# A graph layer and a ternary feed-forward layer on one core: ten weight groups made ternary by GpSimd, and a new order around the last neighbour sums and the first units

## The chip, the cores and the metric

One core of a Trainium2 chip runs the whole program. The time is the device time of one execution in microseconds (us), and of several runs the median is quoted. Engines are named as in the profile: PE is TensorE (PEld its weight loads), DVE is VectorE, ACT is ScalarE, POOL is GpSimd and SP is SyncE, whose queue issues most DMAs.

## What is computed

Inputs are x (1250 nodes x 512), 20000 edges src to dst sorted by dst, two 512 x 512 matrices and a bias for the graph layer, and three weight matrices for the feed-forward layer (gate and up 1408 x 512, down 512 x 1408), all float32.

```python
# graph layer, on xl = layernorm(x)
neigh = segment_sum(xl[src], dst) / maximum(deg, 1)
h = xl @ W_self + neigh @ W_neigh + b
h = where(h >= 0, h, 0.01 * h)
x = x + h / maximum(sqrt(sum(h * h, axis=1)), 1e-12)
# feed-forward layer, on xl = layernorm(x); every weight matrix quantized in groups of 128:
scale = mean(abs(group)) + 1e-5
wq = clip(round(group / scale), -1, 1) * scale
x = x + (silu(xl @ wq_gate.T) * (xl @ wq_up.T)) @ wq_down.T
```

## The kernel before

Everything is written out by hand: each engine's program is one Python function that emits instructions in order, and engines meet only through counting semaphores. Each engine executes its own list strictly in order. The nodes lie in NT = 10 tiles of 125 rows.

**The first stretch, 80 slots.** For each tile PE multiplies the normalized and transposed x (xnT) with W_neigh and W_self (w_sb), eight products of 512 columns, one a slot. Between them it builds the adjacency matrix a_t (1250 x 1250 counts) from one-hot rows: 157 chunks of 128 edges, two a slot. DVE makes the one-hot rows, hot_dst (add_chunk on PE waits for each) and, for eight chunks at once, hot_src. ACT copies finished blocks from PSUM into a_t, the products into y_hi and z, and the transposed x into xnT; DVE makes y_lo, the rest that y_hi leaves. The weights are quantized in the same slots. SP loads them in 34 loads of up to four groups (128 x 128) into four slots of raw; 22 of gate and up, 12 of down. For each group (a job) ACT takes magnitudes and their sum (abs_of: mag, absum), POOL makes a threshold for a load (scales_of: thr), and DVE makes the ternary weight times its magnitude (ternary_of), of which only the sign is used later:

```python
nc.vector.scalar_tensor_tensor(out=tq_of(j), in0=mag_of(j), scalar=thr[:, j:j + 1], in1=raw_of(j),
                               op0=ALU.is_gt, op1=ALU.mult).then_inc(ternary, 1)
```

There are two slots of mag, so ACT's first job of load l waits until the ternaries of load l - 2 are made, and SP's load l until those of l - 4. Loads 0 to 22 are made in the slots, loads 23 to 33 in the neighbour sums.

**The neighbour sums, n = 0 to 9.** PE multiplies a_t with y_hi and y_lo (ten pairs of 512 columns a tile, banks 4 and 5 in turn). POOL has added the bias to z. DVE reads the sum (neighbour_sum: z), applies the leaky step (leak), makes the inverse norm of tile n - 1 and adds it to x (residual: nrm, inv, x_sb, then bn and mv, the statistics), finishes the normalization factors of tile n - 2 (shift1), makes x1_lo of tile n - 3 and the ternaries of the loads that ACT did in n - 1 (down_jobs). ACT squares z, takes roots and normalizes x (normalize1: xn) for tile n - 2; PE transposes tile n - 3 behind tile n, and ACT and DVE split it into x1_hi and x1_lo.

**The units, n = 0 to 32 and three more.** A unit is a row f of 128 hidden features and a third c of the nodes (376, 376 or 500 columns). Each has eight pieces, G0 to G3 and U0 to U3 (one group of gate or up each, x1_hi and x1_lo), and four pieces D0 to D3 (down), which come three units later. The pieces go through seven banks (RING); the matmul of a piece waits until the piece seven before is taken from its bank. ACT takes G0, U0, D1 and D3 and DVE the others, both times nscale. ACT makes silu (sg), POOL the product hh, ACT h_hi and POOL h_lo. The signs of the weights of row f are made by ACT (ternary_out) from a transposition, of row 0 through bank 7 by PE, of most others by DMA. Bank 7 also takes the transpositions of tiles 7, 8 and 9; the table BANK7 says after which piece each comes.

## Time and profile before

| | |
|---|---|
| median of 3 runs | 340.61 us (340.24 to 342.66) |
| the profiled execution | 338.97 us, its span 337.2 us |
| PE busy | 317.1 us (94%) |
| DVE busy | 299.7 us (89%) |
| ACT busy | 236.9 us (70%) |
| POOL busy | 169.3 us (50%) |

The span runs from the first to the last instruction of the profile, and what lies around it makes up the 1.8 us to the time of that execution. Busy times of PE come from modelled ends of pipelined matmuls, so they say where PE has gaps, and not how fast it works. Everything below is from this one execution.

### The profile page before, as it was taken

To read this page: it belongs to the slowest core of one execution; us is meant where nothing else is said; L and a number is where in the kernel's file an instruction comes from. 1 tells how busy PE (TensorE), PEld (TensorE's weight loads), DVE (VectorE), ACT (ScalarE), POOL (GpSimd) and SP (SyncE) were. 2 spreads that over 40 slices of the span, in tenths; PEclk is the share of its full clock that TensorE was granted. 3 is DMA by queue.
4 is the path that set the end of the run, shared out by engine and by line. 5 is a ranking of instruction groups with operands and counts; after the bars stand their busy time and mean duration, and the time that the engine had idled before them with its cause. 6 is when DMAs were issued, how large, how long until landed. Compare 5 with 4: busy or idle time off the path is not lost.

```text
span 337.2 us, 5722 instructions
## 1 busy us (share of the span) xinstructions
PE 317.1 (94%) x1521; PEld 239.6 (71%) x1521; DVE 299.7 (89%) x782; ACT 236.9 (70%) x636; POOL 169.3 (50%) x235
## 2 busy tenths in 40 slices
PE   8999999999999998889879999999999999999991
PEld 3444455454555786668659898998989988899981
DVE  3699999999994399998799999999999999999993
ACT  2188988789882357864778786867878688676750
POOL 6025000010102950100015596989889897899992
PEclk9999999999999999999979999999999999999998
DMA  7992322232320021311001111111110100000305
GB/s 211 285 233 68 91 62 65 65 92 83 84 82 25 4 62 54 90 27 24 9 21 25 27 24 29 24 25 28 24 26 16 23 2 1 2 1 1 118 7 182
DMA packets 23610, 19.62 MB, mean 58 GB/s; under 512 B 15230, under 2 KB 16084, under 8 KB 23576
## 3 DMA queue, kind: packets, MB, share of 16 engines
q1 hardware_dynamic: 23498, 19.16, 21.4%
q8 instruction: 13, 0.21, 0.3%
q14 instruction: 21, 0.17, 0.2%
q10 hardware_dynamic: 78, 0.08, 0.1%
HBM read 13.73 MB, written 2.56 MB: 48 GB/s over the span
## 4 chain that ended last, share of the span: by engine, by line
PE 56%; DVE 25%; issue 6%; POOL 5%; DMA 3%; ACT 2%; SPq 1%; DVEq 0%; ACTq 0%; POOLq 0%
PE bank L1409 44%; DVE hot_dst L1098 4%; PE bank L1306 4%; POOL z L719 4%; DVE tq_gu L999 4%; DVE tq_d L999 3%; PE bank L1343 3%; DMA x_sb<-in_x 3%; DVE hot_src L1089 2%; DVE bn L985 1%; DVE bn L1154 1%; DVE x_sb L1151 1%; PE bank L1258 1%; PE bank L1247 1%; DVE z L1133 1%
## 5 line engine op out<-in xcount | busy, mean ns | idle before, releaser
L1409 PE MATMUL bank<-x_hi,t_gu 128*128 128x376 f32 (+1 forms) x264 | 94.8, 359 | 1.5 <-ACT t_gu L875 0.8
L1409 PE MATMUL bank<-x_lo,t_gu 128*128 128x376 f32 (+1 forms) x264 | 93.5, 354 | 0.0
L1306 PE MATMUL bank<-w_sb,xnT 128*125 128x512 f32 x160 | 82.9, 606 | 0.5 <-ACT z L823 0.3
L1206 DVE SCALAR_TENSOR_TENSOR g_acc<-bank,nscale,g_acc 128x376 f32<-128x376 f32 (+1 forms) x99 | 64.0, 646 | 4.6 <-PE bank L1409 3.2
L1206 DVE SCALAR_TENSOR_TENSOR u_acc<-bank,nscale,u_acc 128x376 f32<-128x376 f32 (+1 forms) x99 | 63.8, 645 | 0.2 <-issue 0.2
L732 POOL TENSOR_TENSOR acc<-acc,d_one 128x376 f32<-128x376 f32 (+1 forms) x58 | 63.6, 1101 | 0.0
L679 POOL TENSOR_SCALAR thr<-absum 128x4 f32<-128x4 f32 (+1 forms) x34 | 9.6, 282 | 98.3 <-ACT mag_early L789 74.6
L742 POOL TENSOR_TENSOR hh<-sg,u_acc 128x376 f32<-128x376 f32 (+1 forms) x32 | 35.2, 1100 | 45.2 <-ACT sg L926 45.1
L1409 PEld LDWEIGHTS bank<-x_hi,t_gu 128*128 128x128 f32 x264 | 50.3, 191 | 6.6 <-issue 1.0
L1409 PEld LDWEIGHTS bank<-x_lo,t_gu 128*128 128x128 f32 x264 | 50.3, 190 | 3.4
L1258 PEld LDWEIGHTS bank<-hot_dst,hot_src 128*126 128x126 bf16 x157 | 20.6, 135 | 40.7 <-DVE hot_dst L1098 25.8
L1409 PE MATMUL bank<-h_hi,t_d 128*128 128x376 f32 (+1 forms) x132 | 47.4, 359 | 0.1
L1409 PE MATMUL bank<-h_lo,t_d 128*128 128x376 f32 (+1 forms) x132 | 46.6, 353 | 0.0
L1343 PE MATMUL bank<-y_hi,a_t 125*125 125x512 f32 x100 | 40.1, 401 | 0.8 <-DVE a_t L1055 0.8
L1206 DVE SCALAR_TENSOR_TENSOR acc<-bank,nscale,acc 128x376 f32<-128x376 f32 (+1 forms) x62 | 39.4, 643 | 0.5 <-POOL acc L732 0.5
L1343 PE MATMUL bank<-y_lo,a_t 125*125 125x512 f32 x100 | 39.4, 394 | 0.0
L751 POOL TENSOR_TENSOR h_lo<-hh,h_hi 128x376 fp32r<-128x376 f32 (+1 forms) x32 | 35.1, 1098 | 3.1 <-ACT h_hi L948 2.5
L905 ACT ACTIVATE d_one<-bank,nscale 128x376 f32<-128x376 f32 (+1 forms) x58 | 34.8, 604 | 1.7 <-PE bank L1409 1.7
L1098 DVE TENSOR_SCALAR hot_dst<-iota_w,key 128x140 bf16<-128x140 uint16 (+4 forms) x150 | 34.5, 271 | 0.9 <-PE bank L1258 0.8
L789 ACT ACTIVATE mag_early<-raw 128x128 f32<-128x128 f32 x92 | 27.5, 304 | 7.7 <-DVE tq_gu L999 6.5
L999 DVE SCALAR_TENSOR_TENSOR tq_gu<-mag_early,thr,raw 128x128 bf16<-128x128 f32 x88 | 28.9, 354 | 2.8 <-POOL thr L679 2.7
L905 ACT ACTIVATE g_acc<-bank,nscale 128x376 f32<-128x376 f32 (+1 forms) x33 | 20.0, 607 | 16.0 <-PE bank L1409 15.2
(140 smaller groups left out, 545.6 us busy)
## 6 DMA issues: line engine op xcount, KB each, us to landing
raw<-in_L_ffn_w_gate SPq DMA_DIRECT2D x11, 256.0 KB, 2.7
raw<-in_L_ffn_w_up SPq DMA_DIRECT2D x11, 256.0 KB, 2.6
out_x<-x_sb SPq DMA_DIRECT2D x10, 224.0 KB
raw<-in_L_ffn_w_down SPq DMA_DIRECT2D x8, 256.0 KB, 2.6
turned<-tq_gu SPq DMA_TRANSPOSE x80, 2.4
w_sb<-in_L_gnn_W_neigh SPq DMA_DIRECT2D x1, 1024.0 KB, 6.1
w_sb<-in_L_gnn_W_self SPq DMA_DIRECT2D x1, 1024.0 KB, 7.6
x_sb<-in_x SPq DMA_DIRECT2D x2, 448.0 KB
```

The source lines that it names most:

```text
L732: nc.gpsimd.tensor_tensor(to, to, d_one[:, o, slot, 0:width(u)], ALU.add).then_inc(d_added, 1)
L742: nc.gpsimd.tensor_tensor(hh[:, u % 2, 0:w], sg[:, u % 2, 0:w], u_acc[:, u % 2, 0:w], ALU.mult).then_inc(h_done, 1)
L751: nc.gpsimd.tensor_tensor(h_lo[:, u % h_slots, 0:w], hh[:, u % 2, 0:w], h_hi[:, u % h_slots, 0:w].bitcast(F32), ALU.subtract).then_inc(hlo ...
L789: nc.scalar.activation(mag_of(j), raw_of(j), ACT.Abs, accum_out=absum[:, j:j + 1]).then_inc(abs_done, 1)
L905: nc.scalar.activation(to, bank_of(u, what)[:, 0:width(u)], ACT.Copy, scale=nscale[:, j:j + 1]).then_inc(act_took, 1)
L999: nc.vector.scalar_tensor_tensor(out=tq_of(j), in0=mag_of(j), scalar=thr[:, j:j + 1], in1=raw_of(j), op0=ALU.is_gt, op1=ALU.mult).then_inc ...
L1098: nc.vector.tensor_scalar(to, numbers, key[:, c:c + 1], None, ALU.is_equal).then_inc(hot_made, 1)
L1206: nc.vector.scalar_tensor_tensor(out=to, in0=bank_of(u, what)[:, 0:w], scalar=nscale[:, j:j + 1], in1=to, op0=ALU.mult, op1=ALU.add).then_ ...
L1258: nc.tensor.matmul(bank[k % 3][0:TQ, 0:NT * WIN].rearrange("p (s d) -> p s d", d=WIN)[:, :, lo:hi], hot_src[:, c // SB % SBS, c % SB, 0:TQ ...
L1306: last = nc.tensor.matmul(to[0:TP, :], xnT[:, t, k * TP:(k + 1) * TP], w_sb[:, k, half * D:(half + 1) * D], start=k == 0, stop=k == KD - 1)
L1343: last = nc.tensor.matmul(bank[4 + n % 2][0:TP, :], a_t[0:TP, s, n * TP:(n + 1) * TP], y[:, s, :], start=s == 0 and y is y_hi, stop=s == N ...
L1409: last = nc.tensor.matmul(bank_of(u, what)[:, 0:width(u)], w, parts[h], start=h == 0, stop=h == 1)
```

## The change

POOL makes the ternaries of ten of the 34 loads, 38 of 132 groups, in two steps (ternary_group); everybody who waited for the counter of ternaries now waits for two counters (wait_ternary). POOL's bias additions are dealt out over the tiles. In the neighbour sums PE's transpositions come a tile later, inside the tile after its first three pairs. DVE makes the residuals of tiles 7 and 8 in their own turn, and POOL that of tile 9. The signs of row 0 go to a place of their own (t_gu0), over data of the edges that are no longer used, where they are made before the last sum is read. RING and BANK7 change, and ACT's takes, normalizations and splits at the start of the units come in another order; DVE's inverse norm of tile 9 comes after the take of G2, and its statistics in unit 1.

```diff
+    t_gu0 = place("t_gu0", [P, 2, D], F32R, "small", edge_data)
+        POOL_LOADS = (6, 10, 14, 18, 22, 24, 26, 28, 30, 32)
+
+        def wait_ternary(engine, j):
+
+            done = [l for l in range(len(loads)) if load_end[l] <= j]
+            assert load_end[done[-1]] == j
+            mine = sum(loads[l][1] for l in done if l not in POOL_LOADS)
+            pools = sum(l in POOL_LOADS for l in done)
+            engine.wait_ge(ternary, mine)
+            if pools:
+                engine.wait_ge(ternary_pool, pools)
-        RING = [2, 6, 4, 5, 3, 1, 0]
+        RING = [2, 6, 4, 1, 0, 5, 3]
-        BANK7 = {(0, "U2"): ("T", 1, 0), (0, "U3"): ("X", 7), (1, "U2"): ("X", 8), (1, "U3"): ("T", 0, 1), (2, "U1"): ("X", 9),
+        BANK7 = {(0, "U2"): ("T", 1, 0), (0, "G1"): ("X", 7), (2, "U0"): ("X", 8), (2, "U3"): ("T", 0, 1), (3, "G0"): ("X", 9),
+            def ternary_group(l):
+
+                n = loads[l][1]
+                js = slice(load_end[l] - n, load_end[l])
+                if l < 2 * NF:
+                    to = tq_gu[:, l, :]
+                else:
+                    o, f = down_order[js.start - 2 * NF * KD]
+                    to = tq_d[:, o, f * P:(f + n) * P]
+                mag = (mag_early if l < LOADS1 else mag_late)[:, l % MAGS, 0:n * P]
+                pool.wait_ge(scales, l + 1)
+                for i, j in enumerate(range(js.start, js.stop)):
+                    m = mag[:, i * P:(i + 1) * P]
+                    nc.gpsimd.tensor_scalar(m, m, thr[:, j:j + 1], None, ALU.is_gt).then_inc(mags_over, 1)
+                pool.wait_ge(mags_over, sum(loads[p][1] for p in POOL_LOADS if p <= l))
+                nc.gpsimd.tensor_tensor(to, mag, raw[:, l % RAWS, 0:n * P], ALU.mult).then_inc(ternary_pool, 1)
...
-            for t in range(NT):
+            def add_bias(t):
+
                 pool.wait_ge(z_out, t + 1)
                 nc.gpsimd.tensor_tensor(z[:, t, :], z[:, t, :], bias_b[0:TP, :], ALU.add).then_inc(z_done, 1)
-            for l in range(LOADS1, len(loads)):
-                scales_of(l)
+
+            for t in range(4):
+                add_bias(t)
+            for n in range(NT):
+                if n + 4 < NT:
+                    add_bias(n + 4)
+                for l in down_loads_in(n):
+                    scales_of(l)
+                    if l in POOL_LOADS:
+                        ternary_group(l)
...
+            t = NT - 1
+            pool.wait_ge(inv_done, 2 * t + 2)
+            nc.gpsimd.tensor_scalar(z[:, t, :], z[:, t, :], inv[0:TP, t:t + 1], None, ALU.mult).then_inc(h_unit, 1)
+            pool.wait_ge(h_unit, 1)
+            nc.gpsimd.tensor_tensor(x_sb[:, t, :], x_sb[:, t, :], z[:, t, :], ALU.add).then_inc(x1_done, 1)
...
+                    if s == 3 and n >= 4:
+                        transpose_x1(n - 4)
...
-                if 3 <= n:
-                    t = n - 3
-                    if t >= 2:
-                        pe.wait_ge(xlo_done, t - 1)
-                    transpose_xn(t, normed1, x1_bank(t), x1n_T, place_of(t)[2])
-                if n == NT - 2:
+                if n == NT - 1:
+                    transpose_x1(n - 3)
+                if n == NT - 3:
                     pe.wait_ge(rdeg_done, 4)
                     ternary_in(0, 0)
```

On POOL, from the last thresholds of the first stretch on (thr) through the bias additions (z) into the down loads: before,

```order
L679 TENSOR_SCALAR thr<-absum 128x4 x19
L719 TENSOR_TENSOR z<-z,bias_b 125x512 x10
L679 TENSOR_SCALAR thr<-absum 128x3
L679 TENSOR_SCALAR thr<-absum 128x4 x2
L679 TENSOR_SCALAR thr<-absum 128x3
L679 TENSOR_SCALAR thr<-absum 128x4 x3
L679 TENSOR_SCALAR thr<-absum 128x3
```

and now, beginning with the product of load 22,

```order
L722 TENSOR_TENSOR tq_d<-mag_early,raw 128x512
L766 TENSOR_TENSOR z<-z,bias_b 125x512 x5
L705 TENSOR_SCALAR thr<-absum 128x3
L705 TENSOR_SCALAR thr<-absum 128x4
L720 TENSOR_SCALAR mag_late<-mag_late,thr 128x128 x4
L722 TENSOR_TENSOR tq_d<-mag_late,raw 128x512
L766 TENSOR_TENSOR z<-z,bias_b 125x512
L705 TENSOR_SCALAR thr<-absum 128x4
L705 TENSOR_SCALAR thr<-absum 128x3
L720 TENSOR_SCALAR mag_late<-mag_late,thr 128x128 x3
```

The additions of tiles 5 and later stand behind a load's comparisons and product, and so do the thresholds of the next loads.

On ACT, from the reading of the last sums to the first units (x_hi is the split of a tile, bank,ss the square, sd a root, xn a normalization, t_gu the signs of a row, g_acc and u_acc the takes): before,

```order
L851 ACTIVATE xn<-x_sb,shift,rs_125 125x512
L875 ACTIVATE t_gu<-bank 128x1024
L859 ACTIVATE x_hi_84<-bank 128x4x125
L890 ACTIVATE bank,ss<-z 125x512
L892 ACTIVATE nrm<-ss 125x1
L845 ACTIVATE sd_124<-mv_123,eps 125x1
L851 ACTIVATE xn<-x_sb,shift,rs_125 125x512
L905 ACTIVATE g_acc<-bank,nscale 128x376
L905 ACTIVATE u_acc<-bank,nscale 128x376
L851 ACTIVATE xn<-x_sb,shift,rs_125 125x512
```

and now,

```order
L936 ACTIVATE t_gu_110<-bank 128x1024
L912 ACTIVATE xn<-x_sb,shift,rs_126 125x512
L906 ACTIVATE sd_125<-mv_124,eps 125x1
L920 ACTIVATE x_hi_84<-bank 128x4x125
L946 ACTIVATE g_acc<-bank,nscale 128x376
L946 ACTIVATE u_acc<-bank,nscale 128x376
L965 ACTIVATE bank,ss<-z 125x512
L967 ACTIVATE nrm<-ss 125x1
L920 ACTIVATE x_hi_84<-bank 128x4x125
L912 ACTIVATE xn<-x_sb,shift,rs_126 125x512
L946 ACTIVATE g_acc<-bank,nscale 128x376
L946 ACTIVATE u_acc<-bank,nscale 128x376
```

The signs of row 0 stand ahead of the last square and no longer next to it, and the takes of unit 0 stand ahead of that square.

On DVE, from the residual of tile 8 on: before,

```order
L1139 SCALAR_TENSOR_TENSOR z<-z 125x512
L1151 SCALAR_TENSOR_TENSOR x_sb<-z,inv,x_sb 125x512
L1154 BN_STATS bn<-x_sb 125x6
L1156 BN_AGGR mv_123<-bn 125x2
L1161 RECIPROCAL rs_125<-sd_124 125x1
L1163 SCALAR_TENSOR_TENSOR shift<-mv_123,rs_125 125x1
L1169 TENSOR_TENSOR x_lo_87<-bank,x_hi_84 128x4x125
L1161 RECIPROCAL rs_125<-sd_124 125x1
L1163 SCALAR_TENSOR_TENSOR shift<-mv_123,rs_125 125x1
L1206 SCALAR_TENSOR_TENSOR g_acc<-bank,nscale,g_acc 128x376
L1206 SCALAR_TENSOR_TENSOR u_acc<-bank,nscale,u_acc 128x376
L1206 SCALAR_TENSOR_TENSOR g_acc<-bank,nscale,g_acc 128x376
```

and now,

```order
L1235 SCALAR_TENSOR_TENSOR x_sb<-z,inv,x_sb 125x512
L1241 BN_STATS bn<-x_sb 125x6
L1243 BN_AGGR mv_124<-bn 125x2
L1208 SCALAR_TENSOR_TENSOR z<-bank,rdeg,z 125x512
L1214 SCALAR_TENSOR_TENSOR z<-z 125x512
L1248 RECIPROCAL rs_126<-sd_125 125x1
L1250 SCALAR_TENSOR_TENSOR shift<-mv_124,rs_126 125x1
L1256 TENSOR_TENSOR x_lo_87<-bank,x_hi_84 128x4x125
L1303 SCALAR_TENSOR_TENSOR g_acc<-bank,nscale,g_acc 128x376
L1303 SCALAR_TENSOR_TENSOR u_acc<-bank,nscale,u_acc 128x376
L1303 SCALAR_TENSOR_TENSOR g_acc<-bank,nscale,g_acc 128x376
L1226 TENSOR_SCALAR nrm<-nrm 125x1
```

The residual of tile 8 and its statistics stand ahead of the last sum's z, and the inverse norm of tile 9 between the takes of unit 0; its x_sb is gone to POOL.

## Rows read from the trace of the kernel before

**Rows 1.** Busy us of each engine by stretch; then PE's clock, DMA.
```profile
19.15:107.50 88.35, 85.31 (x346) 43.28 (x345) 81.30 (x330) 73.23 (x263) 12.55 (x35) 1.00 0.31 84
122.60:163.70 41.10, 37.24 (x177) 28.70 (x177) 37.47 (x113) 27.99 (x109) 2.41 (x10) 1.00 0.21 55
163.70:177.80 14.10, 10.89 (x50) 9.14 (x51) 12.68 (x31) 11.16 (x22) 1.99 (x2) 0.88 0.07 15
```
**Rows 2.** Waits, 15 to 107.5 us: us in all, times, longest.
```profile
PEld bank L1258 <- DVE hot_dst L1098: 25.8, 66, 1.2
...
ACT mag_early L789 <- DVE tq_gu L999: 6.5, 8, 2.0
```
**Rows 3.** Chain that ended last, 133 to 163 us: start, us, what.
```profile
133.33 2.10 DVE tq_d L999 x8
...
141.22 0.66 DVE z L1133
...
147.26 0.66 DVE z L1133
...
152.24 4.68 PE bank L1343 x20
156.92 0.43 PE bank L1247 x4
157.35 0.45 PE bank L1325 x8
```
**Rows 4.** Waits, 107.5 to 163.7 us.
```profile
PEld bank L1247 <- DVE x_lo L1169: 3.4, 3, 1.3
PE bank L1247 <- ACT xn L851: 3.1, 5, 0.9
```
**Rows 5.** Timelines of PE and DVE in the first units.
```profile
163.72 0.41 PE L1409 MATMUL bank<-x_hi,t_gu 128*128 128x376 f32 x1 [0.78 <-ACT t_gu L875]
173.52 1.04 PE L1247 MATMUL bank<-ident,xn 125*128 125x125 f32 x4 [2.46 <-DVE x_lo L1169]
171.20 0.75 DVE L1151 SCALAR_TENSOR_TENSOR x_sb<-z,inv,x_sb 125x512 f32<-125x512 f32 x1
```
**Rows 6.** DVE's timeline while POOL adds the bias.
```profile
113.28 1.12 DVE L1139 SCALAR_TENSOR_TENSOR z<-z 125x512 f32<-125x512 f32 x1
...
117.99 0.67 DVE L1139 SCALAR_TENSOR_TENSOR z<-z 125x512 f32<-125x512 f32 x1
118.58 1.78 DVE L1151 SCALAR_TENSOR_TENSOR x_sb<-z,inv,x_sb 125x512 f32<-125x512 f32 x1
```
**Rows 7.** DVE beside POOL in the first stretch, 22 to 29 us.
```profile
22.70 0.57 DVE L999 SCALAR_TENSOR_TENSOR tq_gu<-mag_early,thr,raw 128x128 bf16<-128x128 f32 x1
23.20 0.34 DVE L999 SCALAR_TENSOR_TENSOR tq_gu<-mag_early,thr,raw 128x128 bf16<-128x128 f32 x1
26.66 0.36 DVE L1098 TENSOR_SCALAR hot_dst<-iota_w,key 128x140 bf16<-128x140 uint16 x1
29.26 0.25 DVE L1098 TENSOR_SCALAR hot_dst<-iota_w,key 128x140 bf16<-128x140 uint16 x1
```
**Rows 8.** POOL's own durations.
```profile
107.58 2.54 POOL L719 TENSOR_TENSOR z<-z,bias_b 125x512 f32<-125x512 f32 x2 [10.65 <-issue]
25.75 0.66 POOL L697 TENSOR_SCALAR win_lo<-win_lo 128x157 f32<-128x157 f32 x1
26.37 0.60 POOL L698 TENSOR_SCALAR win_hi<-win_hi 128x157 f32<-128x157 f32 x1
147.65 0.31 POOL L723 TENSOR_SCALAR nscale<-absum 128x132 f32<-128x132 f32 x1
```
**Rows 9.** Timelines of ACT and DVE behind the first units.
```profile
173.24 1.28 ACT L926 ACT_TABLE_LOAD   x1
176.58 0.61 ACT L878 ACTIVATE t_d<-turned 128x512 fp32r<-128x512 bf16 x1
181.45 0.60 DVE L1206 SCALAR_TENSOR_TENSOR g_acc<-bank,nscale,g_acc 128x376 f32<-128x376 f32 x1
```

More of the change, by code:

```diff
@@ L356, in gnn_ffn, with down_loads_in @@
         NL = len(loads) - LOADS1
+        def down_loads_in(n):
+            lo, hi = (LOADS1 + max(0, min(NL, 2 * i)) for i in (n, n + 1))
+            return range(lo, hi)
         def down_jobs(n):
[L360 to L361 removed]
+            ls = down_loads_in(n)
+            return range(load_end[ls.start - 1], load_end[ls.stop - 1])
         UNITS = [(0, 0), (0, 1), (1, 0), (1, 1), (0, 2), (1, 2)]
@@ L456, in gnn_ffn, with gate_up @@
         t_done = sem("t_done")
+        def gate_up(f):
+            return t_gu[:, t_slot[f], :, :] if f else t_gu0[:, :, :]
         def sg_of(u):
@@ L615, in _ @@
                 if i < TURN_SLOTS:
-                    sp.wait_ge(ternary, load_end[len(loads) - RAWS + i])
+                    wait_ternary(sp, load_end[len(loads) - RAWS + i])
                 else:
@@ L898, in _ @@
                     abs_of(j)
-            def take(u, what, to):
-                if took[u, what] == 1:
-                    act.wait_ge(nscales, 1)
-                act.wait_ge(piece_ready, index[u, what] + 1)
-                j = job_of(u, what)
-                nc.scalar.activation(to, bank_of(u, what)[:, 0:width(u)], ACT.Copy, scale=nscale[:, j:j + 1]).then_inc(act_took, 1)
+                if n == NT - 2:
+                    ternary_out(0, 0)
+                    normalize1(n - 1)
+                    root_of(n)
+                if n == NT - 1:
+                    x1_high(7)
+                    normalize1(n - 1)
             for n in range(NU + LAG):
-                if n < NU:
+                if 0 < n < NU:
                     w = width(n)
@@ L943, in _ @@
                         ternary_out(*BANK7[n - 1, "U3"][1:])
-                    if what == "D2" and 1 <= n <= NU:
-                        act.wait_ge(h_done, u + 1)
-                        if u >= h_slots:
-                            act.wait_ge(piece_ready, index[u - h_slots, "D0"] + 1)
-                        nc.scalar.activation(h_hi[:, u % h_slots, 0:wu], hh_of(u), ACT.Copy).then_inc(hhi_done, 1)
-                if n == 1:
+                    if what == "D2" and 2 <= n <= NU:
+                        high_of_h(u)
+                if n == 2:
                     ternary_out(0, 1)
+                    x1_high(9)
                 elif n in (3, 4) and (n, "U3") in BANK7:
@@ L1220, in _ @@
                         take(u, what)
+                    if n == 0 and what == "G2":
+                        inverse_norm(NT - 1)
                     if n == 1 and what == "U1":
+                        statistics1(NT - 1)
+                        x1_low(7)
                         shift1(NT - 1)
@@ L1319, in ternary_in @@
             def ternary_in(f, down):
-                pe.wait_ge(ternary, JOBS if down else JOBS1)
+                wait_ternary(pe, JOBS if down else JOBS1)
                 if not down:
```

89 lines of the change are left out of this document (63 added, 26 removed).

## The prediction

> **What bounds the kernel now.** I read the stages first. In [rows 1] the reader sees TensorE (PE) busy 85.31 of 88.35 us in the stretch of the products and one-hot chunks, 37.24 of 41.10 us in the neighbour sums from tile 3 on, and 10.89 of 14.10 us in the first units. PE has its gaps in these three, before 177.8 us, and what is gained there moves the whole rest forward. VectorE (DVE) stands nearly level with PE in the first stretch (81.30 of 88.35 us) and in the first units.
>
> Then the waits. In the first stretch PE's weight loads wait for DVE's one-hot rows 66 times, 25.8 us in all, though most of one such wait lies under the matmul before it (PE itself has only 3.0 us without work there); DVE hardly waits, ScalarE (ACT) waits 6.5 us for DVE's ternaries [rows 2]. In the neighbour sums the chain of waits [rows 3] runs on DVE: eight ternaries 2.10 us (0.2625 each), and from one sum (141.22) to the next (147.26) 6.04 us, while PE's tile needs 4.68 us and a transposition 0.43. PE waits there for xn and x_lo, 3.1 and 3.4 us [rows 4]. In the first units two waits end last: 0.78 us for the signs of row 0, which ACT may make only when the last sum has left a_t, and 2.46 us for x_lo behind DVE's x_sb of tile 9 (171.20) [rows 5]. Behind that idle time the granted clock is 0.88 over the stretch: the weaker level, 1.2 GHz, for part of it.
>
> **The first stretch (19 to 107.5 us).** Five groups (loads 6, 10, 14, 18, 22) leave DVE: 20 ternaries by 0.2625. The fifth comes at 97 us, where DVE has time. For each of the other four DVE saves 4 x 0.2625 = 1.05 us. What it pays is read from the lock between DVE and POOL. While POOL adds the bias, DVE's leak takes 1.12 us once and 0.67 us when it got in first, and the x_sb behind it 1.78 us against 0.75 with POOL idle [rows 6, 5]: it stood for the rest of POOL's addition, and the addition then stood for it. In the one-hot stretch a ternary beside POOL's small tensor_tensor took 0.57 us against 0.34 [rows 7]. So a POOL tensor_tensor stops DVE for its own length. Its price: two of 512 columns in 2.54 us, 1.25 us each [rows 8]. POOL's tensor_scalar is not shown with a pointer and is_gt; the nearest rows are is_ge of 157 columns, 0.62 us from start to start, and two-operation arithmetic of 132 columns, 0.31 us [rows 8]. I take 0.5 us for 128 columns, as it is nearer to the comparison (ends 0.31 and 0.62). What it costs DVE has no plain row: from nothing to its whole 0.5 us; a one-hot row beside such an is_ge took 0.36 us against 0.25, so I take 0.1. A group on POOL is then thr 0.2, 4 x 0.5, 1.25 and some waiting for DVE's operations, about 4.2 us. The next group's thresholds stand behind it in POOL's queue. ACT makes 1.2 to 1.6 magnitudes a slot of 1.08 us, so the next group is complete 2.7 to 3.6 us later, and DVE finds its threshold up to 0.8 us late. ACT's magnitudes of load l + 2 wait for POOL as well, and behind them in ACT's queue stand y_hi, xnT, z and the copies into a_t, for which PE waits next.
>
> Each group so costs DVE 1.25 + 0.4 + 0.8 - 1.05 = +1.4 us, four of them +5.6. DVE is idle 88.35 - 81.30 = 7.05 us in this stretch [rows 1], which takes up most of it. If on the other hand DVE gains, PE can gain no more than its 3.0 us. I take **+0.5 us**, ends -2.5 and +6.
>
> The Trainium skill (SBUF — State Buffer, section "SBUF: two separate sides") says that the pair of ports shared by VectorE and GpSimd is an exclusive lock, taken for a whole instruction, against a VectorE operation with two SBUF inputs or in a 2-port mode. The waits just read agree with it for tensor_tensor; the 0.36 us row speaks against it for tensor_scalar. By the rule in full the four comparisons of each group cost DVE their whole length too; that is the slower rival below.
>
> **The neighbour sums.** POOL now makes five bias additions and then one a tile, in place of ten in a row; loads 24, 26, 28, 30 and 32 become POOL's (18 ternaries off DVE); PE's transposition of tile n - 3 behind tile n becomes one of tile n - 4 behind three of tile n's ten pairs, 6 x 0.234 = 1.4 us later. Without the ten additions ahead of them thresholds come at about 117.5 us and not at 121.6. DVE's pace falls from 6.04 to 6.04 - 4 x 0.2625 = 5.0 us a tile, PE's own is 4.68 + 0.43 = 5.1. Nothing but PE left: from tile 3 at 122.6 us seven tiles 32.8, seven transpositions 3.0, row 0's 0.45 [rows 3] make 36.2, and the first unit begins at 158.9 us in place of 163.72: 4.9 us less, which includes the 0.78 us for t_gu, since the signs go into t_gu0 in dead edge data at tile 8. But the lock works here too. POOL has 1.25 (bias) + 0.4 (thr) + 2.0 + 1.25 = 4.9 us of work a tile, nearly always at work, and DVE's leak, x_sb and four ternaries all read two SBUF tiles. If each run of them meets one POOL operation, DVE's pace is about 6.2 us; POOL's loop (ACT's four magnitudes 1.2, thr, comparisons, product, then ACT again) is 5 us bare and 6 with waits. Then z of tile 6 comes at 122.6 + 4 x 6.2 = 147.4, as now, and the first unit gains only what follows it, about 2 us; at worst 1. I take **-3.3 us**, ends -4.9 and -1.
>
> **The first units.** Tile 8's residual and statistics (0.75 + 0.7 + 0.1 us) leave the time behind the last sum, x_sb of tile 9 goes to POOL as two operations (512 columns, about 0.7 and 1.25 us), six takes of 0.52 us no longer stand ahead of it, and the transpositions move. I followed the new order with durations of this trace from the first unit's start, g. DVE takes its first piece at g + 2.3, has the inverse norm at 4.3, POOL x_sb at 6.5; statistics 7.5, root 7.9, the table load 1.28 us [rows 9], silu of unit 0 until 9.8. ACT then goes on with x1_high 0.47, two takes (the second waits for POOL's hh) to 11.3, normalize of tile 9 to 12.0, h_hi to 12.5, silu of unit 1 to 12.9. POOL's h_lo and hh follow, 1.0 us each, to 14.5, h_hi of unit 1 to 15.0, and only then row 0's down signs: before, they were done before the takes of unit 2 (176.58 [rows 9]), now they stand behind h_hi of unit 1, until g + 15.6. PE's D1 of unit 0 waits for them, some 2.5 us, and DVE's x_lo of tile 9 for x1_high behind them. The take of unit 3's G1 comes at g + 16.7. Before it was at 181.45 - 163.72 = g + 17.7. **-1.0 us**, ends -3.1 (DVE's own work alone, 14.6) and +1 (PE's new idle time brings the lower clock into a stretch where PE has 12 pieces a unit and no slack).
>
> **Sum.** +0.5 - 3.3 - 1.0 = -3.8 us against the profiled execution's 338.97 us: 335.2. That execution lies 1.6 us under the median of 340.61, so the median comes to **336.8 us**. Behind 177.8 us the same instructions stand in the same order and should take the same time.
>
> **Rivals.** (1) The relief is given in full: PE sets the pace in the sums, the first units cost what DVE works there, the first stretch gains 1: -1 - 4.9 - 3.1 = -9, so 331.6. For it: PE waits for DVE in every stage. Against: 36 comparisons and ten products of POOL lie in just the stages in which DVE is fullest. (2) The first stretch gives back what the sums win: DVE stopped by each product and late for each following threshold. +4.5 - 3.3 - 1.0: 340.8, no change to be measured. For it: DVE has 8% of slack and PE 3%. (3) Slower: the lock holds DVE for the comparisons too. Then a group costs 1.25 + 2.0 + 0.8 - 1.05 = +3.0 us, four +12, less the 7.05 idle +5; ACT's later copies +1; the sums gain only 1 and the first units nothing: +4.5 to +5, so 345. It decides from about 0.4 us of DVE's time for a comparison on. Against it stands the 0.36 us row. (4) The signs of row 0 are on time after all (POOL's chain shorter than I have it): 334.5, inside the forecast's own range.
>
> **Chances.** Forecast (with rival 4) 0.5, 333.5 to 339; rival 1 0.15; rival 2 0.2; rival 3 0.15. The range goes from rival 1 to most of rival 2 and the lower side of rival 3: 331.5 to 343.5. A measurement of this kernel tells 1%, 3.4 us, from no change: under 337.2 lie rival 1 and over two thirds of the forecast, 0.51; above 344.0 most of rival 3, 0.14; between them 0.35.
>
> **What would show it.** The profile after should have DVE's x_sb and ternaries lengthened at POOL's products (over 1 us at times), and one-hot rows beside POOL's comparisons at most 0.1 us longer; if these are 0.5 longer, rival 3 is true. The last neighbour sum should be read near 160 us, the first unit begin at 159 to 161 with no wait for t_gu; z to z 5.1 to 5.6 us would be PE's pace, 6.2 the lock's. D1 of unit 0 should show a wait for t_d of 2 to 3 us. The first read of the bias stage (107.5 us) should lie within 2 us of where it was; if it is at 110 or later, the first stretch was mis-sized. PE from unit 3 to the end should take as long as now.

## The result, and the profile after

The changed kernel takes 345.61 us in the median (344.87 to 348.04, five runs) against 340.24 for the kernel before in the same series (five runs): the ratio is 1.0168, 95% interval 1.013 to 1.0206. It is slower: the medians are 5.4 us apart, and the ratio makes it 5.7. The forecast was 336.8, its range ended at 343.5, and slower by over 1% had a chance of 0.14. The profiled execution of after is the longest of its five, 348.04 us.

Windows of the same engines and columns as [rows 1] (busy us of PE, PEld, DVE, ACT and POOL; PE's clock). First before and then after, from DVE's first y_lo to the first neighbour sum (the window of [rows 1] begins 2.25 us earlier); then 41.1 us of after's sums and 14.1 us from its first unit on, as long as before's.

```profile
21.40:107.50 86.10, 83.06 (x336) 42.10 (x336) 79.83 (x325) 72.01 (x256) 12.55 (x35) 1.00 0.29 79
```
```profile
24.20:114.20 90.00, 85.97 (x339) 42.87 (x337) 75.76 (x305) 73.20 (x259) 33.42 (x60) 0.98 0.24 68
129.50:170.60 41.10, 38.11 (x177) 29.83 (x176) 38.80 (x96) 26.62 (x108) 22.91 (x33) 0.96 0.20 55
170.60:184.70 14.10, 11.48 (x63) 9.45 (x64) 13.41 (x31) 11.17 (x22) 3.99 (x4) 1.00 0.06 13
```

DVE is relieved in the first stretch, from 79.8 us to 75.8, and yet the stretch is 3.9 us longer: DVE's idle time in it has grown from 6.3 to 14.2 us. POOL has 33.4 us of work there instead of 12.6.

Waits of after from 24 to 114.2 us, which answer to [rows 2] (DVE's own from before stands first), then three of 114.2 to 170.6 us, which answer to [rows 4]:

```profile
DVE tq_gu L999 <- POOL thr L679: 2.7, 4, 0.8
```
```profile
PEld bank L1356 <- DVE hot_dst L1173: 27.5, 63, 1.9
...
DVE tq_gu L1074 <- POOL thr L705: 8.0, 6, 3.0
...
ACT mag_early L850 <- POOL tq_gu L722: 3.1, 4, 1.3
...
PE bank L1356 <- DVE hot_dst L1173: 2.8, 7, 1.1
DVE y_lo L1157 <- POOL tq_d L722: 2.6, 1, 2.6
```
```profile
ACT mag_late L850 <- issue: 7.1, 3, 2.8
PEld bank L1345 <- DVE x_lo L1256: 3.7, 2, 2.6
PE bank L1345 <- ACT xn L912: 2.9, 2, 2.2
```

The longest wait of PE's weight loads for one-hot rows has grown from 1.2 to 1.9 us [rows 2]. DVE waits 8.0 us for thresholds where it waited 2.7. It also waits 2.6 us for the product of load 22 ahead of y_lo of tile 8, a wait that before does not have. The timeline of after at the longest wait for a threshold, where POOL's product stops nothing, because DVE stands idle beside it:

```profile
92.43 1.26 POOL L722 TENSOR_TENSOR tq_gu<-mag_early,raw 128x512 bf16<-128x512 f32 x1
...
93.78 0.19 POOL L705 TENSOR_SCALAR thr<-absum 128x4 f32<-128x4 f32 x1
...
94.01 0.35 DVE L1074 SCALAR_TENSOR_TENSOR tq_gu<-mag_early,thr,raw 128x128 bf16<-128x128 f32 x1 [2.98 <-POOL thr L705]
```

The chain that ended last in the neighbour sums of after, against [rows 3]:

```profile
133.08 1.99 DVE tq_d L1074 x4
...
139.56 2.33 DVE tq_d L1074 x4
141.89 0.66 DVE z L1208
...
153.58 2.32 DVE tq_d L1074 x4
155.89 0.66 DVE z L1208
```

Four ternaries now take as long as eight did (2.10 us [rows 3]). The timeline of after shows why at the first of these places, POOL's product of 384 columns beside them:

```profile
133.00 2.06 DVE L1074 SCALAR_TENSOR_TENSOR tq_d<-mag_late,thr,raw 128x128 bf16<-128x128 f32 x4
133.90 1.02 POOL L722 TENSOR_TENSOR tq_d<-mag_late,raw 128x384 bf16<-128x384 f32 x1
```

Four ternaries are 1.05 us, and 1.05 + 1.02 = 2.07. Two tiles later a group's ternaries meet the product and the bias addition behind it, and take 3.00 us:

```profile
146.09 3.00 DVE L1074 SCALAR_TENSOR_TENSOR tq_d<-mag_late,thr,raw 128x128 bf16<-128x128 f32 x4
...
146.36 1.01 POOL L722 TENSOR_TENSOR tq_d<-mag_late,raw 128x384 bf16<-128x384 f32 x1
...
147.32 1.34 POOL L766 TENSOR_TENSOR z<-z,bias_b 125x512 f32<-125x512 f32 x1
```

ACT begins its next magnitudes only at 149.16, right behind them; that is the wait of 2.8 us in the list above.

**Stretches of all runs.** To keep the start of the program out of it, whose length changes from one execution to the next (the first y_lo comes between 20.2 and 24.2 us, in after's profile at 24.2, in before's at 21.4), I cut each profile into three by rows of DVE: from the start of the first y_lo to that of the last one (the first stretch), from there to the last read of a sum (L1208 in after: the neighbour sums), and from there to the end of the span (the units). Each is from one execution. The lengths repeat: the first stretch is 85.95 to 86.12 us in the eight profiles that have it as before, the sums 54.7 to 54.8 in eight that have the new order and no group there. The ratios are of timed runs to those of before.

| kernel | ratio to before (95%) | first stretch | sums | units |
|---|---|---|---|---|
| before | | 86.0 | 55.2 | 174.7 |
| after | 1.0168 (1.013 to 1.0206) | 89.9 | 57.3 | 174.9 |
| e1 order only | 0.9955 (0.9931 to 0.9979) | 86.0 | 54.8 | 174.8 |
| e2 first five | 1.0109 (1.0074 to 1.0143) | 90.0 | 54.8 | 175.1 |
| e3 down five | 1.0047 (1.0021 to 1.0073) | 86.1 | 57.3 | 173.3 |
| e4 POOL only | 1.01 (1.0064 to 1.0137) | 90.0 | 55.9 | 174.6 |
| e5 threshold first | 1.0143 (1.0096 to 1.0191) | 90.5 | 54.8 | 174.6 |
| e6 unused comparisons | 1.0026 (1.0 to 1.0052) | 87.2 | 54.8 | 176.0 |
| e7 unused products | 1.0168 (1.0132 to 1.0203) | 92.2 | 54.7 | 176.0 |
| e8 signs early | 0.9922 (0.9894 to 0.995) | 86.0 | 54.7 | 172.6 |
| e9 tiny groups | 1.0 (0.9974 to 1.0025) | 84.6 | 56.1 | 175.2 |
| e10 down, comparisons | 0.9974 (0.9948 to 0.9999) | 86.0 | 55.0 | 174.9 |
| e11 residual on DVE | 0.9954 (0.9924 to 0.9984) | 86.1 | 54.8 | 173.4 |
| e12 down, products | 1.0096 (1.0063 to 1.0129) | 86.0 | 58.2 | 173.5 |
| e13 ten loads cheap | 0.9829 (0.9798 to 0.986) | 84.8 | 53.5 | 172.6 |
| e14 all loads cheap | 0.9729 (0.9695 to 0.9762) | 83.1 | 51.7 | 172.8 |
| e15 x_lo of 6 first | 0.9898 (0.9857 to 0.994) | 86.0 | 54.8 | 172.7 |
| e16 split products | 1.0072 (1.0045 to 1.0098) | 91.3 | 54.9 | 172.4 |

The profiled pair differs by 9.1 us: 2.8 at the start, 4.0 in the first stretch, 2.1 in the sums, 0.2 in the units. The 2.8 are of that one execution; the other 6.3 stand beside 5.4 us between the medians. PE's clock is not what makes the stretches longer: it is 0.98 in after's first stretch but 1.00 in that of e7, which is longer still, and 0.97 in after's sums but 1.00 in those of e3, which are as long.

### The profile page after: what moved, and what is told of

It reads as the page before. It is cut to its first block, busy times and chain, and to the rows that moved or that the text cites. A ratio compares the mean times of both kernels' runs of the same rounds, so it can differ in the third digit from the quotient of the medians.

```text
span 346.3 us, 5759 instructions
## 1 busy us (share of the span) xinstructions
PE 322.9 (93%) x1521; PEld 242.2 (70%) x1521; DVE 296.8 (86%) x743; ACT 237.1 (68%) x636; POOL 210.6 (61%) x285
## 3 DMA queue, kind: packets, MB, share of 16 engines
q1 hardware_dynamic: 23498, 19.16, 20.2%
## 4 chain that ended last, share of the span: by engine, by line
PE 61%; DVE 18%; ACT 7%; issue 5%; POOL 5%; DMA 1%; SPq 1%; ACTq 1%; DVEq 0%; POOLq 0%
PE bank L1511 41%; PE bank L1404 10%; PE bank L1448 4%; DVE hot_dst L1173 2%; PE bank L1356 2%; DVE tq_d L1074 2%; DVE tq_gu L1074 2%; POOL mag_early L720 2%; ACT mag_early L850 1%; DMA e_i<-in_dst 1%; ACT mag_late L850 1%; DVE z L1208 1%; DVE bn L1241 1%; DVE z L1214 1%; DVE x_sb L1235 1%
## 5 line engine op out<-in xcount | busy, mean ns | idle before, releaser
L1404 PE MATMUL bank<-w_sb,xnT 128*125 128x512 f32 x160 | 87.2, 634 | 2.5 <-DMA w_sb<-in_L_gnn_W_neigh 2.1
L705 POOL TENSOR_SCALAR thr<-absum 128x4 f32<-128x4 f32 (+1 forms) x34 | 11.8, 347 | 72.5 <-ACT mag_early L850 63.4
L1448 PE MATMUL bank<-y_hi,a_t 125*125 125x512 f32 x100 | 41.2, 412 | 0.8 <-DVE a_t L1130 0.8
L1448 PE MATMUL bank<-y_lo,a_t 125*125 125x512 f32 x100 | 40.4, 404 | 0.0
L1356 PE MATMUL bank<-hot_dst,hot_src 128*126 128x140 bf16 (+6 forms) x157 | 27.9, 260 | 2.9 <-DVE hot_dst L1173 2.8
```

Of the source, the lines that this page charges most:

```text
L1356: nc.tensor.matmul(bank[k % 3][0:TQ, 0:NT * WIN].rearrange("p (s d) -> p s d", d=WIN)[:, :, lo:hi], hot_src[:, c // SB % SBS, c % SB, 0:TQ ...
L1404: last = nc.tensor.matmul(to[0:TP, :], xnT[:, t, k * TP:(k + 1) * TP], w_sb[:, k, half * D:(half + 1) * D], start=k == 0, stop=k == KD - 1)
L1448: last = nc.tensor.matmul(bank[4 + n % 2][0:TP, :], a_t[0:TP, s, n * TP:(n + 1) * TP], y[:, s, :], start=s == 0 and y is y_hi, stop=s == N ...
```

## Experiments: which half costs

Here and below the edits are to the changed kernel unless another is named.

**e1, e2, e3.**

```diff
-        POOL_LOADS = (6, 10, 14, 18, 22, 24, 26, 28, 30, 32)
+        POOL_LOADS = ()                      # e1
+        POOL_LOADS = (6, 10, 14, 18, 22)     # e2
+        POOL_LOADS = (24, 26, 28, 30, 32)    # e3
```

> The changed kernel with no weight group made ternary by POOL (POOL_LOADS empty): VectorE makes all of them, and only the new order of the tile steps and of the first units is left. Theory A (POOL's groups cost the time, the order is worth something): below the kernel before, 337 to 340 us, neighbour sums of 5.1 to 5.8 us a tile. Rival B (the order itself costs, half clock and row 0's late down signs): 342 to 346 us, as the changed kernel.

> The changed kernel with POOL making only the five groups of the first stretch (loads 6, 10, 14, 18, 22); the down weights are VectorE's again. Theory A: the groups of the first stretch hold most of the loss, so 3 to 5 us above the kernel with the order alone, and the first neighbour sum at 111 to 114 us of the trace. Rival B (the loss is in the neighbour sums): within 1 us of the kernel with the order alone.

> The changed kernel with POOL making only the five groups of the down weights (loads 24 to 32). Theory A: the first stretch is as before (first neighbour sum at 107.5 us), and the time is within 1.5 us of the kernel with the order alone. Rival B (groups of two cost as much as they relieve, since VectorE's ternaries beside them take 0.5 instead of 0.26 us, and ScalarE waits): 2 to 4 us above it.

**e4** is the kernel before with the ten groups on POOL (ternary_group, wait_ternary) in its own order.

> The kernel before with POOL making the ten groups, in its own order of steps (all bias adds, then the scales). Theory A: the two parts of the change add up, so this is the kernel before plus 5 to 8 us. Rival B (the groups are harmless without the new order): within 1.5 us of the kernel before.

The order alone is 0.9955 of before, a gain of 1.5 us (338.23 against 339.76). The first five groups add 1.0109 - 0.9955 = 1.5%, 5.2 us, of which the profiles show 4.0 in the first stretch (90.0 against 86.0) and nothing in the sums. The five down groups add 0.9%, 3.1 us, of which the profiles show 2.5 in the sums (57.3 against 54.8); that is rival B of e3. Together that makes 0.9955 + 0.0154 + 0.0092 = 1.0201, a little above the 1.0168 measured. So the groups on POOL are the loss, and the order is not (rival B of e1 falls). e4 costs 1.0%, 3.4 us, less than theory A had: the same 4.0 us in the first stretch, but only 0.7 in the sums. Its bias additions are all over before the down groups, and only two DVE rows of its sums, one of 1.10 and one of 1.56 us, are stopped by a product; after has five such ternaries. Why the old order spares the others was not tested.

## Experiments: what a group costs in the first stretch

**e5, to e2.** The next load's threshold ahead of the product:

```diff
+                if l + 1 < LOADS1:
+                    scales_of(l + 1)    # and no longer in the loop over the loads
                 pool.wait_ge(mags_over, ...)
                 nc.gpsimd.tensor_tensor(to, mag, ...)
```

> The kernel with the first five groups alone on POOL, and the thresholds of the next group computed between the comparisons and the product of a group instead of behind the product, so they come 1.3 us earlier. Theory A (VectorE waits for thresholds that stand behind the group's work in POOL's queue): 1.5 to 3 us below the kernel with the first five groups, that is 340 to 341.7 us, and the waits of the group tq_gu for thr, 8 us over six times in the changed kernel, fall below 4. Rival B (the lock of the shared port during comparisons and product is the price): within 0.7 us of the kernel with the first five groups.

**e6 and e7, to e1.** Behind the thresholds of seven loads POOL computes what nobody reads:

```diff
+        BESIDE = (6, 8, 10, 12, 14, 16, 18)
+                for i in range(4):    # e6
+                    nc.gpsimd.tensor_scalar(to[:, i * P:(i + 1) * P], w_sb[:, 0, i * P:(i + 1) * P],
+                                            thr[:, j:j + 1], None, ALU.is_gt)
+                nc.gpsimd.tensor_tensor(to, w_sb[:, 0, 0:RW], w_sb[:, 1, 0:RW], ALU.mult)    # e7
...
```

> The kernel with the new order and no group on POOL, to which POOL gets 28 comparisons whose results are never used (7 sets of four, 128x128, of the weights W_neigh with the thresholds, into rows of tq_gu that are overwritten later). They fit between two thresholds, so no threshold comes late by more than 0.3 us. Theory A: the comparisons hold VectorE up by at most 0.1 us each, so the time rises by 0 to 1.5 us over the kernel with the order alone (338.2), since VectorE has some idle time. Rival B (a comparison locks VectorE out for all of its 0.6 us): 17 us of lock, of which at least half shows, so +5 us or more.

> The kernel with the new order and no group on POOL, to which POOL gets 7 products of 128x512 whose results are never used. Theory A (late thresholds are the price): each locks VectorE out for at most 1.3 us, 9 us in all spread over 55 us, of which VectorE's idle time there takes a part: +1 to +4 us over the kernel with the order alone. Rival B (the products' lock alone explains the five groups' 4.9 us): +6 us or more for seven, 0.9 us each and more.

The threshold that comes earlier gives nothing: 90.5 us against 90.0, ratio 1.0143 against 1.0109 (the intervals overlap). My leading theory was that DVE's 8 us of waits for thresholds are the loss and that moving the threshold gets it back; it does not. The timeline of e5 shows what happens: the threshold is there 1.3 us before the product ends, DVE starts the ternary, and the product stops it.

```profile
89.68 0.19 POOL L705 TENSOR_SCALAR thr<-absum 128x4 f32<-128x4 f32 x1
89.91 1.46 DVE L1077 SCALAR_TENSOR_TENSOR tq_gu<-mag_early,thr,raw 128x128 bf16<-128x128 f32 x1 [1.86 <-POOL thr L705]
89.96 1.26 POOL L724 TENSOR_TENSOR tq_gu<-mag_early,raw 128x512 bf16<-128x512 f32 x1
```

e7 prices such a stop without any group: seven products make the stretch 92.2 - 86.0 = 6.3 us longer, 0.90 us each of their 1.26 to 1.76, and each lengthens a DVE row by 0.8 to 1.1 us. Its timeline, at one of them: a DVE row of 0.34 us becomes 1.43, and PE then waits for the one-hot row behind it.

```profile
42.43 1.43 DVE L1086 SCALAR_TENSOR_TENSOR tq_gu<-mag_early,thr,raw 128x128 bf16<-128x128 f32 x1
42.45 1.27 POOL L730 TENSOR_TENSOR tq_gu<-w_sb 128x512 bf16<-128x512 f32 x1
...
44.85 0.29 PE L1368 MATMUL bank<-hot_dst,hot_src 128*126 128x180 bf16 x1 [0.50 <-DVE hot_dst L1185]
```

28 comparisons (0.60 us in the changed kernel, here 0.60 to 1.55) make it 87.2 - 86.0 = 1.3 us longer, 0.05 us each. Grouped by form, DVE's rows beside them are hardly longer than in e1, here e1 and then e6 (busy us, mean ns of one):

```profile
L1074 DVE SCALAR_TENSOR_TENSOR tq_gu<-mag_early,thr,raw 128x128 bf16<-128x128 f32 x88 | 28.5, 348 | 2.8 <-POOL thr L705 2.7
```
```profile
L1090 DVE SCALAR_TENSOR_TENSOR tq_gu<-mag_early,thr,raw 128x128 bf16<-128x128 f32 x88 | 28.9, 353 | 2.8 <-POOL thr L706 2.3 <-DVE flag L1202 0.4
```

By the timed runs e6 is 0.7% (2.4 us) above e1, more than the stretch shows and more than theory A had, and e7 2.1% (7.2 us); the units of both profiles are some 1.1 us longer than e1's, at a lower clock (the section on the first units has it). Rival B of e7 holds as a price: where products stop DVE, 0.9 us each is lost. Rival B of e6, and with it rival 3 of the prediction as a mechanism, is false: 353 ns for 348 is no lock. The Trainium skill (SBUF — State Buffer, "SBUF: two separate sides") has any GpSimd operation that reads SBUF and starts first hold a VectorE operation with two SBUF inputs for its whole length. For tensor_tensor the two timelines above agree; for this comparison e6's means do not.

**What the five groups cost in the changed kernel is mostly not such a stop.** DVE's waits for POOL in the first stretch, from e1, e2, e5 and e16 (which cuts each product in four, see below), in windows that end at the last y_lo:

```profile
DVE tq_gu L1074 <- POOL thr L705: 2.7, 4, 0.8
```
```profile
DVE tq_gu L1074 <- POOL thr L705: 8.4, 6, 3.2
DVE y_lo L1157 <- POOL tq_d L722: 2.6, 1, 2.6
```
```profile
DVE tq_gu L1077 <- POOL thr L705: 4.6, 5, 1.9
DVE y_lo L1160 <- POOL tq_d L724: 2.4, 1, 2.4
```
```profile
DVE tq_gu L1079 <- POOL thr L705: 8.9, 6, 3.3
DVE y_lo L1162 <- POOL tq_d L726: 2.5, 1, 2.5
```

| kernel | DVE waits for POOL | DVE rows longer beside a product | first stretch |
|---|---|---|---|
| e1 | 2.7 us | none | 86.0 |
| e2 | 11.0 us | one, by 0.5 us | 90.0 |
| e5 | 7.0 us | four, by 3.7 us in all | 90.5 |
| e16 | 11.4 us | six, by 0.2 to 0.3 us each | 91.3 |
| e7 | 2.3 us | seven, by 7.1 us in all | 92.2 |

In e2 and in after one product of five stops a DVE row (a one-hot row of 0.78 us). Beside three others DVE stands idle until the threshold comes, and beside the fifth it waits for the product itself. e5 trades 4.0 us of these waits for some 3 us more of stops and is no faster. So the late thresholds and the stops stand in for each other: taking one away leaves the other. e16 has the waits nearly without the stops, and its stretch is the longest of the three with groups.

## Experiments: what the relief of VectorE is worth

**e9.** Comparisons over one column, and a memset for the product:

```diff
-                    nc.gpsimd.tensor_scalar(m, m, thr[:, j:j + 1], None, ALU.is_gt)
+                    nc.gpsimd.tensor_scalar(m[:, 0:1], m[:, 0:1], thr[:, j:j + 1], None, ALU.is_gt)
-                nc.gpsimd.tensor_tensor(to, mag, raw[...], ALU.mult)
+                nc.gpsimd.memset(to, 1.0)
```

> The changed kernel with the work of POOL's ten groups shrunk: the comparisons run over one column, and a memset of the group stands in the product's place, so VectorE is relieved of the 38 ternaries at next to no price (the ten groups' weights are not computed). Theory A (VectorE was worth relieving, and the price on POOL ate it): 2 to 5 us below the kernel with the order alone, that is a ratio to before of 0.981 to 0.990. Rival B (the first stretch and the sums do not depend on these ternaries): within 1 us of the kernel with the order alone, 0.993 to 0.998.

**e13 and e14, to e8** (no group on POOL). In ternary_of, under a condition for the ten loads (e13) or for all from load 4 on (e14):

```diff
+                    nc.vector.memset(tq_of(j), 1.0).then_inc(ternary, 1)
+                    return
```

> The kernel with row 0's signs early, no group on POOL, and in the ten groups' place on VectorE a memset of 128 columns for each ternary (these 38 blocks of the weights are not computed): relief of VectorE with POOL wholly out of it. Theory A (TensorE paces both stretches, so the relief has little to give): first to last y_lo 84.5 to 85.5 us against 86.0, last y_lo to last z within 0.3 us of 54.7, the time 0 to 1.5 us below the kernel with the signs early. Rival B (VectorE paces the sums and the groups' own work hid it): 2 to 4 us below it, the sums at 52 to 53.5 us.

> The same with a memset for the ternaries of all weight groups from the fifth on, three times the relief (nearly all blocks of the weights are not computed). Theory A: the first stretch falls to 82 to 84.5 us and stops there, TensorE busy at 98% or more, the sums at 54.0 to 54.7 us. Rival B: three times what the ten groups gave, 6 us or more in all.

In e13 a DVE row of 0.35 us becomes one of 0.165, 38 times. The 20 of the first stretch (3.7 us of DVE) gain 86.0 - 84.8 = 1.2 us, the 18 of the sums (3.3 us) gain 54.7 - 53.5 = 1.2. So **a microsecond taken off DVE is worth about a third of a microsecond** in either stretch. e9 says the same of the first: 20 ternaries gone, 1.3 us shorter than e1. Its time is above both theories (1.0): its sums are 1.3 us longer than e1's and take back what the first stretch gains; more on that below. Only in e14 PE reaches its own pace in the sums, 51.61 us busy of 51.70 (a window of e14, PE first):

```profile
20.50:103.60 83.10, 81.57 (x336) 42.25 (x335) 66.58 (x325) 71.83 (x256) 10.68 (x35) 1.00 0.28 80
103.60:155.30 51.70, 51.61 (x247) 41.49 (x248) 41.82 (x132) 32.22 (x130) 17.03 (x22) 1.00 0.16 44
```

Both theories were too plain. Of e13, A had the first stretch right, but the sums do gain, 1.2 us, where A had at most 0.3; in time e13 is 0.9% (3.2 us) below e8, within B's range. e14's sums stand at 51.7 where A had at least 54.0; its first stretch is 83.1, inside A's range. The time of e14, 0.9729, is 1.9% (6.6 us) below e8, as B had it, and the two stretches show 2.9 and 3.0 us of that.

For the first stretch a sum comes out near: five products 5 x 0.90 = 4.5, twenty comparisons 20 x 0.045 = 0.9, relief -1.2, in all +4.2; measured +4.0 (e2 against e1). But it gives all five products e7's price of a stop, and in e2 one of them stops a row. An estimate from the table above: without that one, the comparisons and the relief, 4.0 - 0.5 - 0.9 + 1.2 = 3.8 us are left in e2 for 8.3 us more of waiting, a little under half of it; the same working gives 4.1 us for 8.7 in e16, and 1.1 for 4.3 in e5. That the sum meets the measured time is in part luck: a product waited out cost here about what a product that stops DVE costs. ACT's own 3.1 us of waits for POOL's products were not separated from this.

## Experiments: the down groups in the sums

**e10 and e12, to e3.** e10 has e9's memset and whole comparisons, e12 e9's comparisons of one column and whole products.

> The kernel with the five groups of the down weights alone on POOL, their 18 comparisons kept and a memset in the place of each product. Theory A (the product's lock is the price, as in the first stretch): 2 to 4 us below the kernel with the five down groups, ratio to before 0.993 to 0.999. Rival B (POOL's time in the loop abs, threshold, comparisons sets the pace): less than 1.2 us below it, 1.001 to 1.005.

> The kernel with the five groups of the down weights alone on POOL, their comparisons over one column each (so the down weights of these groups are not computed rightly) and the products whole. Theory A (the product's lock is the price): within 1.2 us of the kernel with the five down groups, ratio to before 1.001 to 1.006. Rival B (POOL's 11 us of comparisons in the loop set the pace): 2 to 4 us below it, 0.993 to 0.999.

**e16, to e8 with the ten groups.** Each product cut in four, one behind each comparison:

```diff
+                    if i >= 1:
+                        cols = slice((i - 1) * P, i * P)
+                        pool.wait_ge(mags_over, over + i)
+                        nc.gpsimd.tensor_tensor(to[:, cols], mag[:, cols], raw[:, l % RAWS, cols], ALU.mult)
```

> The kernel with row 0's signs early and all ten groups on POOL as in the changed kernel, but each product of 128x512 cut into four of 128x128, one behind each comparison. Theory A (a lock costs what it exceeds VectorE's lead over TensorE, so pieces of 0.3 to 0.5 us pass within it): the first stretch, 4.0 us longer with whole products, is at most 2 us longer, and the time is 336 to 339.5 us. Rival B (the sum of locked time counts, whatever the pieces): 4 us longer or more, 341 us or more.

Without the products the sums are 55.0 us, with them and hardly any comparison 58.2, with both 57.3: here the price is the product's (theory A; e12's time lies even above its range). In e12 the bias addition behind the product stops a ternary as well, in five tiles (1.37 to 1.38 us each), and in after and e3 in one. In e16 the pieces take 0.45 us each, 1.8 for four against 1.27 for a whole one, and the two stretches answer differently. In the first stretch +5.3 us over e8, more than the +4.0 of whole products: theory A has the stops right, which are 0.2 to 0.3 us, and the time wrong. The number is rival B's, but not for its reason: the stops are 1.5 us in all, and the waits for POOL stay as long as with whole products (11.4 us against e2's 11.0). In the sums 54.9 against 57.3: the pieces pass almost unseen, and the bias additions meet no ternary. The time, 1.0072 of before, is slower than e8 by 1.5%.

e9's sums (56.1) are longer than e10's (55.0), which has more work on POOL, and 2.6 us longer than e13's, which has none. The traces show why: it matters where POOL's bias addition falls. In e9 it stops a ternary in five tiles, the first of them at 121.60 (1.38 us), in e10 in two, in e1 and e13 in none. One of e9's, four ternaries beside it:

```profile
134.04 2.25 DVE L1074 SCALAR_TENSOR_TENSOR tq_d<-mag_late,thr,raw 128x128 bf16<-128x128 f32 x4
134.07 1.28 POOL L766 TENSOR_TENSOR z<-z,bias_b 125x512 f32<-125x512 f32 x1
```

The memsets do not hold DVE: of the twelve ternaries beside e10's five memsets none takes over 0.35 us. No run moved the additions alone.

## Experiments: the first units

In after PE's first down piece waits for row 0's signs, as forecast:

```profile
PE bank L1511 <- ACT t_d L939: 2.5, 1, 2.5
```

**e8, to e1.** The signs ahead of the high half of h of unit 1:

```diff
                     if what == "D2" and 2 <= n <= NU:
+                        if n == 2:
+                            ternary_out(0, 1)
                         high_of_h(u)
                 if n == 2:
-                    ternary_out(0, 1)
                     x1_high(9)
```

> The kernel with the new order and no group on POOL, in which ScalarE's signs of row 0's down weights stand ahead of the high half of h of unit 1 instead of behind it. Theory A (TensorE's wait of 2.5 us for t_d before the first D1 is lost time, and the half clock that follows it too): the wait falls below 0.6 us, 1.5 to 2.5 us less than the kernel with the order alone: 335.7 to 336.7 us. Rival B (another result is late at the same place, x_lo of the last tile or the low half of h): less than 0.7 us less.

**e11, to e8.** The last tile's residual on DVE again (add_residual behind inverse_norm(NT - 1), POOL's two operations gone), and x1_low(7) ahead of statistics1(NT - 1).

> The kernel with row 0's signs early, in which the residual of the last tile is VectorE's again (one instruction of 0.74 us for POOL's 1.6 and 1.3) and x_lo of tile 7 stands ahead of the last tile's statistics. Theory A (TensorE's 1.3 us wait for x_lo of tile 7 came of POOL's slow residual): that wait falls below 0.3 us and the time is 0.5 to 1.3 us less, ratio to before 0.988 to 0.991. Rival B (VectorE sets the pace of the first units, so its added 0.74 us costs what the wait gave): within 0.5 us of 0.992.

**e15, to e8.** In the last turn of the sums leak(n) comes behind x1_low(n - 3).

> The kernel with row 0's signs early, in which VectorE makes x_lo of tile 6 ahead of the leak of the last tile. Theory A (TensorE's 1.15 us wait for that x_lo before unit 0's last product is lost time): 0.4 to 0.9 us below the kernel with the signs early. Rival B (the last tile's chain of leak, norm, residual, statistics and x_hi is the next to be late, by the 0.7 us that the leak comes later): within 0.3 us, or up to 0.7 us above.

The same piece in e1 and then in e8:

```profile
177.84 0.65 PE L1511 MATMUL bank<-h_hi,t_d 128*128 128x376 f32 x1 [2.50 <-ACT t_d L939]
```
```profile
176.37 0.41 PE L1512 MATMUL bank<-h_hi,t_d 128*128 128x376 f32 x1 [0.47 <-DVE g_acc L1304]
```

The units fall from 174.8 to 172.6 us, and by the timed runs e8 is 0.3% (1.1 us) below e1, less than the 1.5 that theory A had at least; the intervals of the two ratios overlap a little. Part of the 2.2 us of the profiles is the clock. From 163 to 190 us it is 0.94 of full speed in e1 and 0.87 in e6 (1.2 GHz, the lower level, for a part of it), and below 1 in e2, e5, e7, e9 and e10 too, but 1.00 in e3 and e12, which have the same wait of 2.52 us. Their units take 173.3 and 173.5 us, so the wait is worth some 0.8 us by itself and the lower level up to 2.6 more (176.0 in e6), when it comes. In the six profiles with the signs early (e8, e11, e13 to e16) the clock is 1.00 throughout.

e11 gives PE the x_lo in time and takes it back at once: where the wait for x_lo was (1.3 us), there is now one for DVE's next take.

```profile
175.08 0.44 PE L1508 MATMUL bank<-x_hi,t_gu 128*128 128x376 f32 x1 [1.07 <-DVE g_acc L1298]
```

Ratio 0.9954 against 0.9922 (the intervals overlap), units 173.4 against 172.6: nothing is gained, nearer to B, though 1.1 us above e8 where B had at most 0.5. The residual can stay on POOL, slow as it is. In e15 the wait for x_lo falls from 1.2 to 0.4 us, another of 0.4 us, for bank 3 behind the later squares, comes after it, and the units are 172.7 against 172.6. The ratio of 0.9898 is not to be told from e8's 0.9922. Both are faster than both kernels: before by 0.8 to 1%, after by 2.4 to 2.7%.

## Why the prediction was wrong

The step that failed is the same in the first two terms: DVE's relief was counted in full, and the price of POOL's groups was set against it and against DVE's idle time. The runs showed that the relief is worth a third of its time, that idle time takes up little of the price, and that part of the price was not in the sum.

- **The neighbour sums, -3.3 taken, +2.1 measured, the largest miss and outside its own ends (-4.9 and -1).** The order without groups gives -0.4 there (e1), and the five groups +2.5 (e3). What failed is "DVE's pace falls from 6.04 to 6.04 - 4 x 0.2625 = 5.0 us a tile": with the groups the reads of two tiles are 14.0 us apart (141.89 to 155.89), 7.0 a tile. The prediction named the lock as what might eat the relief ("z to z 5.1 to 5.6 us would be PE's pace, 6.2 the lock's"), and the lock it was (e10: 55.0 us without the products). But it let each run of DVE's reads meet one POOL operation: four ternaries meet the product and the bias addition behind it (3.00 us at 146.09), and ACT's magnitudes for the next tile start only behind them. The end at -1 did not hold because it priced the lock against the relief in full.
- **The first stretch, +0.5 taken, +4.0 measured (ends -2.5 and +6).** A product was priced at 1.25 us of DVE's time; one that stops DVE costs the stretch 0.90 (e7). A comparison was priced at 0.1 and costs 0.05, though it lasts 0.6 and not 0.5. A group was +1.4 and is +0.8. What failed is "DVE is idle 88.35 - 81.30 = 7.05 us in this stretch, which takes up most of it": the idle time was not used up but grew to 14.2 us. A ternary less was counted at its full 0.2625 us and is worth 0.06. The late threshold, 0.8 us a group, was too small: DVE waits 8.0 us for thresholds instead of 2.7, up to 3.0 at once, and in the changed kernel this wait and not the lock stands beside most products. e5 moved it and gained nothing, because the product then stops DVE. That the fifth group is free was wrong as well: DVE's y_lo of tile 8 waits 2.6 us for its product, a wait that the prediction did not have.
- **The first units, -1.0 taken, +0.2 measured.** The mechanism was right: the wait of D1 for t_d was forecast at 2 to 3 us and is 2.5; t_gu is waited for no more than 0.3 us (e1). The size was off because the clock was put at the range's end and not into the sum; where it stays at 2.4 GHz (e3, e12) the units take 173.3 and 173.5, which is -1.4 and -1.2.
- **Rivals.** The time came out as rival 3 had it (345), by rival 2's mechanism: DVE late for thresholds in the first stretch and stopped by each product in the sums, with the sums added on top instead of paying for it. That it meets rival 3's figure is luck. The 0.36 us row against rival 3 was read rightly. (Rival 1 speaks of 36 comparisons; there are 38.) What the prediction lacked is a case in which the relief is not worth its time anywhere; rivals 1 and 2 and the forecast all paid it out in full.
- **The mark set beforehand** ("if it is at 110 or later, the first stretch was mis-sized") was met: 114.2, and 111.4 without the 2.8 us of that execution's start.

## What to carry to other kernels

Before work is moved from VectorE to GpSimd, price it by what the busier engines lose and gain and not by its own length: here a GpSimd tensor_tensor of 1.27 us with two SBUF inputs lengthened a VectorE row by up to 1.1 us and cost the stretch 0.90, while the ternaries that it took off VectorE gave back a third of their time. Idle time of an engine, as a share, was no buffer here against a stop or a late result of a microsecond or more. Look also at what now stands behind the new work in the queue, and who waits for it. When a wait shows in the trace, ask what takes its place before counting it as a gain: the wait for thresholds turned into stops, and the wait for x_lo of tile 7 into one for DVE's next take. A cause that is replaced when it is taken away was still the cause in the kernel as it ran.
